# The causal mask of an attention kernel's max pass, moved from TensorE's accumulation to a fused VectorE instruction

## The reference, cut to what matters

```python
xn = _layernorm(x)                              # x: (4, 1024, 256)
x = x + attention(xn, Wq, Wk, Wv, Wo) + ffn(xn, ...)

# attention: 16 heads of width 16, rotary q and k
scores = einsum('bhqd,bhkd->bhqk', q, k) / sqrt(16)
scores = where(causal, scores, -1e9)
probs = softmax(scores)
attn = einsum('bhqk,bhkd->bhqd', probs, v) @ Wo.T

# ffn: 9 paths, one chosen per token
idx = argmax(tanh(x_mixed @ Wo1 + bo1) @ Wo2 + bo2)
out = _layernorm(xn + path[idx](x_mixed))
```

## Time and profile before

| | |
|---|---|
| median of 3 runs | 881.25 us (878.26 to 882.08) |
| the profiled execution | 879.47 us, span 877.7 us |
| TensorE matmuls busy | 790.5 us, 90% |
| VectorE busy | 621.8 us, 71% |
| ScalarE busy | 458.2 us, 52% |
| GpSimd busy | 288.4 us, 33% |
| mean granted clock of TensorE | 0.971 of full speed |

### The profile page before, as it was taken

How to read it: one execution, slowest core, us unless ns; L and a number is a source line. 1 busy time by engine, 2 the same in 40 slices (tenths; PEclk the granted TensorE clock), 3 DMA queues, 4 the chain that set the end, 5 groups by cost and what they waited for, 6 DMA issues and landing times.

```text
span 877.7 us, 12898 instructions
## 1 busy us (share of the span) xinstructions
PE 790.5 (90%) x4928; PEld 392.1 (45%) x4928; DVE 621.8 (71%) x1222; ACT 458.2 (52%) x780; POOL 288.4 (33%) x419
## 2 busy tenths in 40 slices
PE   4856979979999989989999998998999999999986
PEld 2522434344455534435455543434455554444434
DVE  5967796667678687567859679676867767766522
ACT  2452534645555644556546654564555564554662
POOL 1001032880515121583332402387051512120513
PEclk9967999999999999989999999999999999999999
DMA  6372323124421434021550623113441241410102
GB/s 216 108 180 47 75 49 53 36 64 123 69 51 31 95 97 73 1 73 64 108 98 1 115 79 76 27 37 100 109 78 21 49 97 30 73 29 1 25 1 72
DMA packets 40575, 59.99 MB, mean 68 GB/s; under 512 B 4813, under 2 KB 36830, under 8 KB 37634
## 3 DMA queue, kind: packets, MB, share of 16 engines
q1 hardware_dynamic: 36002, 54.39, 26.6%
q0 software_dynamic: 4224, 4.19, 3.2%
q10 hardware_dynamic: 288, 0.59, 0.2%
HBM read 42.04 MB, written 16.85 MB: 67 GB/s over the span
## 4 chain that ended last, share of the span: by engine, by line
PE 67%; DVE 19%; POOL 8%; ACT 2%; issue 2%; DMA 2%; SPq 1%; DVEq 0%; ACTq 0%; POOLq 0%
PE bank L1206 13%; PE bank L1187 11%; PE bank L1167 11%; PE bank L1153 8%; DVE piecemax L994 7%; PE bank L1143 5%; PE bank L1105 4%; PE bank L1234 3%; PE bank L1164 3%; PE bank L1116 2%; PE bank L1216 2%; PE bank L1123 2%; DVE stats L855 2%; POOL prob L671 2%; POOL turned L653 2%; POOL raw L654 2%
## 5 line engine op out<-in xcount | busy, mean ns | idle before, releaser
L994 DVE TENSOR_REDUCE piecemax<-bank 128x1 f32<-128x512 f32 (+3 forms) x608 | 380.7, 657 | 178.1 <-PE bank L1167 177.1
L778 ACT ACTIVATE prob<-bank 128x512 f32<-128x512 f32 x576 | 332.6, 596 | 317.6 <-PE bank L1187 313.9
L671 POOL TENSOR_SCALAR_AFFINE_SELECT prob<-prob 128x256 f32<-128x256 f32 (+1 forms) x320 | 132.5, 434 | 417.8 <-ACT prob L778 415.6
L1167 PE MATMUL bank<-k_st,q_st 96*128 96x128 bf16 (+3 forms) x1152 | 231.0, 281 | 11.9 <-DVE piecemax L994 11.7
L1187 PE MATMUL bank<-q_st,k_st 98*128 98x512 bf16 (+3 forms) x768 | 223.6, 333 | 13.9 <-DMA q_st<-shiftT 8.1
L1206 PE MATMUL bank<-prob,v_sb 128*17 128x512 f32 (+3 forms) x1536 | 158.7, 502 | 14.7 <-POOL prob L671 14.7
L1167 PEld LDWEIGHTS bank<-k_st,q_st 96*128 96x128 bf16 x1152 | 99.2, 100 | 146.2 <-issue 52.7
L1187 PEld LDWEIGHTS bank<-q_st,k_st 98*128 98x128 bf16 x768 | 71.5, 99 | 116.1 <-ACT prob L778 57.6
L1153 PE MATMUL bank<-w_sb,mid 128*128 128x256 f32 (+1 forms) x320 | 85.4, 390 | 2.2 <-DVE z L987 2.2
L1105 PE MATMUL bank<-xnT,wqk_sb 128*128 128x512 f32 x128 | 68.5, 637 | 5.2 <-ACT xnT L725 3.7
L1143 PE MATMUL bank<-xm,w_sb 128*128 128x512 f32 x128 | 67.5, 609 | 0.0
(11 more groups left out here) (82 smaller groups left out, 672.9 us busy)
## 6 DMA issues: line engine op xcount, KB each, us to landing
scratch<-parts SPq DMA_DIRECT2D x16, 768.0 KB, 3.8
q_st<-scratch SPq DMA_DIRECT2D x90, 128.0 KB, 6.9
k_st<-scratch SPq DMA_DIRECT2D x15, 384.0 KB, 4.8
z<-in_x SPq DMA_DIRECT2D x8, 512.0 KB, 4.6
mask<-chosen SPq DMA_DIRECT2D x16, 256.0 KB
z<-in_x POOLq DMA_DIRECT2D x8, 512.0 KB, 6.0
out<-z SPq DMA_DIRECT2D x8, 512.0 KB, 3.2
k_st<-scratch SPq DMA_DIRECT2D x15, 256.0 KB, 5.4
```

The lines of the kernel that those rows point to most:

```text
L671: nc.gpsimd.affine_select(out=d, in_=d, compare_op=ALU.is_ge, fill=0.0, base=0, pattern=pattern, channel_multiplier=-1).then_inc(masked, 1)
L778: nc.scalar.activation(prob[:, place_of(G, i), :], ps[:, :], ACT.Exp, scale=float(DK) ** -0.5).then_inc(act_took, 1)
L994: nc.vector.tensor_reduce(piecemax[:, G % 2, t, h:h + len(cols), piece], ps[:, 0:len(cols) * w].rearrange("p (h k) -> p h k", k=w), AX.X, ...
L1167: ins = nc.tensor.matmul(ps[:, k * w:(k + 1) * w], q_st[0:PARTS, G % STACKS, h, t * P:(t + 1) * P], k_st[0:PARTS, G % STACKS, h, k0:k0 + w ...
```

## The change

The max pass is cut otherwise: a unit is one head, one query tile and one half of the keys, up to and with the diagonal block. Tiles 0 to 3 have one unit a head, of 128 to 512 columns; tiles 4 to 7 have two, one of 512 columns without a diagonal and one of 128 to 512 with it. That makes 48 units a group. TensorE's mask matmul is gone, and each unit is one matmul. `causal_sb` is now 512 wide, zeros with the triangle in its last 128 columns; units that hold a diagonal block go through `tensor_tensor_reduce`, which adds the last w columns of it to the bank's w columns, writes the sums back into the bank and their maximum into `piecemax`. The other units keep `tensor_reduce`. `piecemax` has two pieces instead of three, and `req` of the feed-forward's routing shares the tile of the scores.

```diff
-PIECES = 3
+PIECES = 2
...
     for t in range(NT):
-        out.append((t, 0, [(h, t * P, P) for h in range(GH)]))
-        for piece, k0, w in ((1, 0, min(t, HT) * P), (2, HALF, (t - HT) * P)):
-            if w > 0:
-                n = 4 if w == P else 2 if w == 2 * P else 1
-                out += [(t, piece, [(h, k0, w) for h in range(a, a + n)]) for a in range(0, GH, n)]
+        if t >= HT:
+            out += [(t, 0, h, 0, HALF) for h in range(GH)]
+        k0 = t // HT * HALF
+        out += [(t, t // HT, h, k0, (t + 1) * P - k0) for h in range(GH)]
     return out
+
+
+def has_diagonal(u):
+    return MAX_UNITS[u][1] == MAX_UNITS[u][0] // HT
...
-        causal_sb = sb("causal_sb", [P, P], BF16)
+        causal_sb = sb("causal_sb", [P, HALF], BF16)
...
-        req = sb("req", [P, NT, PATHS], F32)
+        req = score_sb
...
-                nc.gpsimd.affine_select(out=causal_sb[:, :], in_=causal_sb[:, :], compare_op=ALU.is_ge, fill=NEG,
-                                        base=0, pattern=[[-1, P]], channel_multiplier=1).then_inc(consts_set, 1)
+                tri = causal_sb[:, HALF - P:HALF]
+                nc.gpsimd.affine_select(out=tri, in_=tri, compare_op=ALU.is_ge, fill=NEG, base=0, pattern=[[-1, P]], channel_multiplier=1).then_inc(consts_set, 1)
...
             def max_unit(G, u):
-                t, piece, cols = MAX_UNITS[u]
-                ps = take(("max", G, u))
-                h, _, w = cols[0]
-                nc.vector.tensor_reduce(piecemax[:, G % 2, t, h:h + len(cols), piece],
-                                        ps[:, 0:len(cols) * w].rearrange("p (h k) -> p h k", k=w),
-                                        AX.X, ALU.max).then_inc(dve_took, 1)
+                t, piece, h, _, w = MAX_UNITS[u]
+                ps = take(("max", G, u))[:, 0:w]
+                to = piecemax[:, G % 2, t, h, piece:piece + 1]
+                if has_diagonal(u):
+                    dve.wait_ge(consts_set, 1)
+                    nc.vector.tensor_tensor_reduce(ps, ps, causal_sb[:, HALF - w:HALF], 1.0, NEG, ALU.add, ALU.max,
+                                                   to).then_inc(dve_took, 1)
+                else:
+                    nc.vector.tensor_reduce(to, ps, AX.X, ALU.max).then_inc(dve_took, 1)
...
             def max_scores(G, u):
-                t, piece, cols = MAX_UNITS[u]
+                t, _, h, k0, w = MAX_UNITS[u]
                 pe.wait_ge(stack_filled[G % STACKS], 16 * FILL_DMAS * (G // STACKS + 1))
                 if G == 0 and t >= HT:
                     pe.wait_ge(second_filled, 16 * FILL_DMAS)
-                ps = begin(("max", G, u))
-                if piece == 0:
-                    nc.tensor.matmul(ps[:, :].rearrange("p (h k) -> p h k", h=GH), ident_bf[:, :],
-                                     causal_sb[:, None, :].to_broadcast([P, GH, P]), start=True, stop=False)
-                for k, (h, k0, w) in enumerate(cols):
-                    ins = nc.tensor.matmul(ps[:, k * w:(k + 1) * w], q_st[0:PARTS, G % STACKS, h, t * P:(t + 1) * P],
-                                           k_st[0:PARTS, G % STACKS, h, k0:k0 + w],
-                                           start=(piece != 0), stop=(piece != 0 or k == len(cols) - 1))
-                ins.then_inc(slot_filled, 1)
+                nc.tensor.matmul(begin(("max", G, u))[:, 0:w], q_st[0:PARTS, G % STACKS, h, t * P:(t + 1) * P],
+                                 k_st[0:PARTS, G % STACKS, h, k0:k0 + w],
+                                 start=True, stop=True).then_inc(slot_filled, 1)
```

More of the change, by code:

```diff
@@ L77 @@
 NSTEPS = SCORE_UNITS[-1][1] + 1
-assert (NM, NS, NSTEPS) == (38, 36, 10)
+assert (NM, NS, NSTEPS) == (48, 36, 10)
 def step_half(step):
```

## The result

The changed kernel takes 878.28 us (median of 20 runs, 872.93 to 881.25) against 880.66 (20 runs, 878.26 to 882.08): ratio 0.9969, 95% interval 0.9956 to 0.9982. The range (862 to 925) held it. In what follows a ratio is always to runs of the kernel before taken beside it, and differences are differences of ratios times 880 us. Where a kernel's bare number is given, it is its median. The prediction gave 0.51 to slower, 0.2 to no change and 0.29 to faster.

The account below looks back on a forecast made before the run. It took TensorE as the bound on average and VectorE as second, coupled through three banks. Mask matmuls -26, max matmuls -10, L994's chain share +10, first group +6, surfacing VectorE work +29 gave +9, forecast 890 us, range 862 to 925.

Parts of the forecast that it names:

- The mask's matmuls, -26: On TensorE, 128 mask matmuls go, 28 us in all; the chain holds 26 us of them, taken as the saving.
- the 50 that were named as a sign: Expected sign in the profile: L1164 gone and TensorE's busy time down by about 50 us.
- The grouping of the max matmuls, -10: On TensorE, 768 max matmuls a run replace 1152 with the same columns; gain 0 to 34 us, 10 taken.
- VectorE's work, +88 us: In the max pass, fused instructions 250 us plus accumulator reads 51 us replace 213 us of reductions.
- I take 0.10: Time in us of each of 512 accumulator reads on VectorE, between bounds of 0.06 and 0.154; 51 us in all.
- What surfaces, +10 and +29: Steady part: L994's chain share grows with the pass, +10 us; part of VectorE's remaining growth surfaces, +29 us.
- 0.4 of the 72 us: Share of VectorE's remaining steady-part growth, which fills its gaps, that becomes time: +29 us; bounds 0.2 and 0.6.
- 3/38 against 3/48 of a group: Slack of TensorE's three max banks before and after, said to hold less than before.
- 30% or more was forecast: Expected sign: VectorE's share of the chain rises from 19% to 30% or more; under 20% means the prediction is wrong.
- The first group, +6: At the start, bound by VectorE: first 16 units +3.3 us, the other 32 +2.8 us, together +6.
- the second, the saving survives: Rival: read costs 0.06, VectorE's work grows 68 us, gaps take most of it; 868 us, down to 855; chance 0.27.
- Two cycles a column: Rival: fused instruction takes two cycles a column reading and writing PSUM, +170 us of work, 1010 us; chance 0.05.

Follow-up runs that it names:

- e1: The kernel before without its 128 mask matmuls, old cut of 38 units and plain reductions kept: 859.38 us, ratio 0.977.
- e3: The changed kernel with 128 mask matmuls of 512 columns put back as overwritten work: 897.23 us, ratio 1.0193.
- e4: The changed kernel's new cut with the mask added by TensorE (512 matmuls of 128 columns) and plain reductions everywhere: 893.89 us, ratio 1.0154.
- e10: e2 with narrow units packed, four 128-wide or two 256-wide heads a bank, 38 units again, no mask: 858.29 us, ratio 0.975.
- e2: The changed kernel with plain reductions in place of all 512 fused instructions, no mask, 48 units a group: 873.07 us, ratio 0.9916.
- e7: e1 with ten two-column memsets a group added on VectorE, one behind every fourth reduction: 859.45 us, ratio 0.9767.
- e9: e1 with two banks for the max units in place of three: 883.95 us, ratio 1.0044.
- e5: The changed kernel with the shift's transposes and placement due 0.04 and 0.08 of a group later, except the first group: 881.5 us, ratio 1.0014.
- e6: The changed kernel with max units due at distances proportional to VectorE's time for them instead of equal distances: 890.76 us, ratio 1.0114.
- e8: e1 with the shift's transposes and placement later, the same edit as e5: 867.25 us, ratio 0.9856.

## Why the prediction missed

**The sign.** It forecast a slowdown of 1%, and the kernel is 0.3% faster. Its sum was -26 - 10 + 10 + 6 + 29 = +9. Measured, TensorE's side is -20 where it had -36, and VectorE's side is +18 (13 for the cut, with its few matmuls fewer, and 5 for the fused instructions) where it had +45, together -2. VectorE's side was 27 us too dear and turned the sign; TensorE's gain was 16 us too large and hid more than half of that. That the number came within 12 us is luck of this kind: with VectorE's work at its measured size and everything else of the sum left (-36 + 4 + 6 + 11) it would have been 866, as far off on the other side. What was right is the form, a saving of TensorE that is eaten by waits for banks.

**The mask's matmuls, -26.** Measured -20 (e1), -20 (e3), -21 (e4). The share of the chain (26 us) was a fourth too high as an estimate, and 0.72 of the work was time. TensorE's busy time fell by 11 us and not by the 50 that were named as a sign: L1164 took 51.5 us with it, the fewer and wider max matmuls are busy 250.5 us in place of 231.0, and L1206, whose work is unchanged, 162.9 in place of 158.7, at the lower granted clock.

**The grouping of the max matmuls, -10.** Measured by e10 against e1: -2, within the intervals of both nothing. Why the sets of four cost so little was not looked into.

**VectorE's work, +88 us.** Measured +33, of which 11 come with the ten more units (620.4 in e1, 631.1 in e2) and 24 with the fused instructions. This is the step that failed first: "I take 0.10: it has no tensor input, but it must wait for the instruction before it, and today's back-to-back reductions overlap ..., which the pair can't do in full." The next fused instruction starts with the read, and a unit costs 0.05 us more than plain, below both bounds of the range given for the read. The main instructions were priced about right by their neighbours (0.29, 0.425, 0.551, 0.689 taken; 0.304, 0.445, 0.577, 0.711 measured), but their lengths overlap, and it is distances that add. The sum set lengths (250 us) against a busy time without the overlaps (212.9). The 16 pairs of the first group, four of each width, show the distance: they start at 44.08 and end at 51.35, 7.3 us, where the sum had 9.4. That is 0.45 us a pair with its read, and 512 such pairs make an estimated 233 us in place of 301.

The Trainium skill ("VectorE: DVE Perf Modes", section on the TRN2 errata), weighed there, would have the four widths at an estimated 235 us. The lengths measured are longer, 2.037 us for the four or 261 us, but the distances of the pairs, with the reads in them, agree with it. The Trainium skill's rule in the same section, that many small tiles pay their latency many times, is told there of sources in SBUF. In this trace the ten more units a group did bring 11 us of VectorE work, and e7 shows that here such work cost nothing.

**What surfaces, +10 and +29.** "I let 0.4 of the 72 us surface." The measured loss is 13 + 5 = 18 us, but not by this way. 9.6 us of pure VectorE work surfaced with 0 (e7), the fused instructions' 24 with 5, and the ten more units with 13. The text had the likeliest cause in half a sentence (3/38 against 3/48 of a group) and used it only to argue for a share of VectorE's work, when it was a term of its own that needs no VectorE work at all (e9). Of the signs named, VectorE's share of the chain came to 25% where 30% or more was forecast and under 20% would have been wrong; the waits went the forecast way, 63 us (79 with the mask matmuls) to 132, and 177 to 140.

**The first group, +6.** The first 16 units took 1.1 us longer than the 11 of before (7.3 against 6.13), not 3.3, and that was not on the path: VectorE then waits for TensorE in both kernels, and its next reduction starts at 58.51 us, before at 58.67. In the trace ScalarE copies group 0's first sum at 89.9 us in place of 89.0 and the second at 133.2 in place of 129.1, so 4 us were lost by the end of the first group, as forecast in kind, in a stretch where TensorE's clock was lower as well (0.8 against 0.9 in the fifth and sixth slice); both spans are 877.7 us, so the rest of the run made up for it.

**The rivals.** The nearest was the second, the saving survives; its condition, a read at its lower bound, came true and more, and still most of the saving was eaten, by the units. Two cycles a column did not come about: 1.06 ns a column, with the result written back into the bank that is read.

**The fastest kernel** is e10, level with e1: 858.29 us, ratio 0.975. It leaves the mask out of the maxima only. Since the maximum is a shift that cancels in the softmax, this changes the result only by rounding, as long as no future key of the same diagonal block outscores all allowed ones by so much that their exponentials vanish; that is a condition on the inputs, which the mask made unnecessary. The move to VectorE was a cheaper mask, and on inputs that meet the condition the cheapest is none.

## What to carry to other kernels

Where two engines hand banks to each other in fixed order, count the units and what each bank holds before pricing the work: a cut into more, emptier banks can cost time even if the receiving engine has time to spare (13 us here, most likely as lead), and losing one bank of three cost more here (24 us) than taking out 28 us of matmuls gained (20). Price an instruction that is new in a queue by the distance from start to start, not by its length: here a second instruction of 141 ns behind it cost at most 0.05 us. And a change of order alone, with the same instructions, moved this kernel by 4 to 13 us (e5, e6, e8), so a change that also alters the order needs a control for it. And before moving a piece of work to another engine, ask whether its result needs it at all.

## What was not expected of the hardware

The accumulator read (141 ns, 512 of them, 72.2 us busy) is recorded beside the fused instruction that follows it: both start at the same time, and pairs are 0.25 us apart at 128 columns. The fused instruction reads a bank, adds an SBUF operand in bf16, writes the sums back into the same bank and keeps the maximum, all at 1.06 ns a column by its lengths ((0.711 - 0.304)/384) and 1.04 by the distances (0.65 and 0.25).
